# Second attention: half of each head's exponentials are added up on GpSimd before VectorE sums them

## The chip, the cores and the metric

The kernel runs on one core of a Trainium2 chip. The metric is the device time of one execution in microseconds (us). A core has five engines that run in parallel, each through its own queue in order: TensorE (PE), VectorE (DVE), ScalarE (ACT), GpSimd (POOL) and SyncE (SP, used for DMAs). They wait for each other through semaphores.

## The reference

A small transformer over x of shape (2, 1024, 256) with a context of 77 rows of 192: a first cross attention, a feed-forward with a token-dependent part, a **second cross attention**, and a mixture of 8 experts that each pick 257 tokens of a batch. Each stage normalises x and adds its result to it. The change concerns the softmax of the second attention:

```python
q = (x @ Wq).reshape(B, Sq, h, d).transpose(0, 2, 1, 3)      # h = 8 heads, d = 64
k = (context @ Wk).reshape(B, -1, h, d).transpose(0, 2, 1, 3) # 77 keys
scores = jnp.einsum('bhid,bhjd->bhij', q, k) * scale
attn = jax.nn.softmax(scores, axis=-1)
out = jnp.einsum('bhij,bhjd->bhid', attn, v)
```

## The kernel before

The 2048 rows of x are 16 tiles of 128 rows. In the second attention a tile n has 8 x 77 = 616 scores per row. Keys and query weights are multiplied together beforehand (`WK`), as are values and output weights (`VW`), so a tile goes through these steps:

1. TensorE, `scores(n)`: 12 products into the PSUM banks 4 and 5, which it may overwrite when VectorE has signalled `v_sub` for tile n-1.
2. VectorE, `scores(n)`: the maximum of each head (L1617), then the subtraction into `Pb[n % 3]` (L1621), which signals `v_sub`.
3. ScalarE, `exps(n)`: the exponential in place (L2232), signals `a_exp`.
4. VectorE, `normed(n)`: the sum of each head's 77 exponentials (L1626) and its reciprocal (L1628), signals `v_rec`.
5. GpSimd, `normed(n)`: multiplies the 616 exponentials by the reciprocals (L2541), signals `g_pb`.
6. TensorE transposes the tile in five pieces (L880) into banks 6 and 7; ScalarE copies the high part out (L1973) and VectorE the rest (L1653).
7. TensorE, `product(n)`: 15 products with `VW`; VectorE adds the result to x (L1634) and takes its statistics (L1636).

Each engine's program is a Python generator, `attention1(g)` for the four tiles of group g. `scores`, the exponential and `normed` run two tiles ahead of the transposes. The function `merge` interleaves the side work into this order, a piece after so many steps: the transposed queries of the next group (`queries`, L1486 on VectorE), the routing of finished tiles (`route_norm`: statistics to mean and variance, L1598 to L1602 on VectorE, a power on GpSimd, L2467, and a product, L2532, then the normalised rows, L1218 on VectorE; `route_pick`: router products L920, a small softmax, L1688 to L1699, and the splitting of the scores into pieces on GpSimd, L2595 to L2603), and in group 0 the routing constants (`constants`, L1706 to L1715 on VectorE and L2560 to L2583 on GpSimd). The order is fixed when the program is built. For GpSimd it is, around the multiplications (m0 to m15): m0, m1, first constants, m2, two iotas, the rest of the constants (which wait for VectorE's L1715), m3 to m6, power and product of routing group 0, m7, m8, m9, splitting of group 0, m10, power and product of group 1, m11, m12, m13, splitting, m14, power and product, m15. For VectorE a tile's turn is maximum and subtraction of tile n+2, L1653 of tile n, addition and statistics of tile n-1, sum and reciprocal of tile n+2.

Of the kernel before, what the change touches and what calls it, by code (L numbers as in the profile page):

```python
# [11 lines left out]
ALU = mybir.AluOpType  # L12
ACT = mybir.ActivationFunctionType
AX = mybir.AxisListType
# [5 lines left out]
H1 = 8  # L20
# [75 lines left out]
def build(nc, A, out, y_dram):  # L96
    with ExitStack() as root:
        def sem(name):
            return root.enter_context(nc.semaphore(name))
# [108 lines left out]
        s3 = Arena(R0.at)  # L208
# [5 lines left out]
        sm = s3("sm", [128, 3, 3, 8])  # L214
# [4 lines left out]
        s3 = Arena(qa_at)  # L219
# [3 lines left out]
        Pb = [s3(f"Pb{i}", [128, 640]) for i in range(3)]  # L223
        PT1 = [[s3(f"PTx{i}{j}", [128, 5, 128], F32R) for j in range(2)] for i in range(2)]
        wr_at = nc.sbuf_usable_end // 64 * 64 - 16384
        yr2 = s3("yr2", [128, 4, D])
        xf2 = s3("xf2", [128, 2, 512])
        assert s3.at <= wr_at


# [107 lines left out]
        g_pb = sem("g_pb")  # L338
# [93 lines left out]
        a_exp = sem("a_exp")  # L432
# [24 lines left out]
        def tensor_program(pe):  # L457
# [8 lines left out]
            def clear(b):  # L466
                if busy[b]:
                    pe.wait_ge(*busy[b])
                    busy[b] = None

            def warm(m, n):

                clear(m)
                for _ in range(n):
                    pe.transpose(bank[m][:, 0:128], ident[:, :], ident[:, :])  # L475
# [360 lines left out]
            def scores(n):  # L836
                g, t = n // 4, n % 4
                b, c = g // 2, 512 * (g % 2) + 128 * t
                clear(4)
                clear(5)  # L840
                if t == 0:
                    pe.wait_ge(v_xt, 2 * (8 + g) + 2)
                if n == 0:
                    pe.wait_ge(v_wk, 8)
                for u in range(2):
                    w_ = slice(308 * u, 308 * u + 308)
                    op = three(bank[4 + u][:, 0:308], [((xt[0][:, k, c:c + 128], xt[1][:, k, c:c + 128]),
                                                        (WK[0][:, b, k, w_], WK[1][:, b, k, w_])) for k in range(2)])
                op.then_inc(p_s, 1)
                busy[4] = busy[5] = (v_sub, n + 1)  # L850

            def product(n):
                b, T, m = n // 8, PT1[n % 2], 1 + n % 2
                K = [128, 128, 128, 128, 104]
                clear(m)
                pe.wait_ge(v_pT, n + 1)
                if n == 0:
                    pe.wait_ge(v_vw, 6)
                three(bank[m][:, 0:256], [((T[0][0:K[c], c, :], T[1][0:K[c], c, :]),
                                           (VW[0][0:K[c], b, c, :], VW[1][0:K[c], b, c, :])) for c in range(5)]).then_inc(p_pv, 1)  # L860
                busy[m] = (v_x1, n + 1)

            def attention1(g):
                if g == 0:
                    scores(0)
                    warm(1, 10)
                    scores(1)
                    yield
                    yield
                for t in range(4):  # L870
                    n = 4 * g + t
                    if n + 2 < NT:
                        scores(n + 2)
                    yield
                    clear(6)
                    clear(7)
                    pe.wait_ge(g_pb, n + 1)
                    o = ps[:, 6:8, :].rearrange("p u n -> p (u n)")
                    for c in range(5):
                        op = pe.transpose(o[:, 128 * c:128 * c + 128], Pb[n % 3][:, 128 * c:128 * c + 128], ident[:, :])  # L880
                    op.then_inc(p_pT, 1)
                    busy[6] = busy[7] = (v_pT, n + 1)
                    yield
                    if n:
                        product(n - 1)
                        yield
                    yield
                if g == 3:
                    product(NT - 1)
# [124 lines left out]
            drain(sd, vw_)  # L1014
            sd = queries(1, q_)
            merge(attention1(0), (sd, 0.6))
            drain(sd)
            for g in range(1, 3):
                qs = queries(g + 1, q_)
                rs_ = both(idle(6 if g == 1 else 3), route_norm(g - 1), idle(3 if g == 1 else 6), route_pick(g - 1, (0,), 0, 0))  # L1020
                merge(attention1(g), (qs, 0.6), (rs_, 1.0))
                drain(qs, rs_)
            rs_ = both(idle(3), route_norm(2), idle(8), route_pick(2, (0, 3), 0, 3))
            merge(attention1(3), (rs_, 1.0), (both(idle(12), route_norm(3)), 1.0))
            last_routes(rs_, route_norm(4), route_pick(3, (4,), 7, 4), route_pick(4, (5,), 6, 5))

# [162 lines left out]
        def vector_program(v):  # L1189
            made = {"st": 0, "unit": 0}  # L1190

            def step(op):

                op.then_inc(v_st, 1)
                made["st"] += 1

            def settle():
                v.wait_ge(v_st, made["st"])
# [424 lines left out]

            def normed(n):
                v.wait_ge(a_exp, 144 + n + 1)
                step(v.tensor_reduce(sm[:, n % 3, 1, :], Pb[n % 3][:, 0:616].rearrange("p (h s) -> p h s", h=H1), AX.X, ALU.add))  # L1626
                settle()
                v.reciprocal(sm[:, n % 3, 2, :], sm[:, n % 3, 1, :]).then_inc(v_rec, 1)  # L1628

# [8 lines left out]
            def attention1(g):  # L1638
                if g == 0:
                    scores(0)  # L1640
                    scores(1)
                    yield
                    normed(0)
                    normed(1)
                    yield
                src = ps[:, 6:8, :].rearrange("p u n -> p (u n)")[:, 0:640].rearrange("p (c n) -> p c n", c=5)
                for t in range(4):
                    n = 4 * g + t
                    if n + 2 < NT:
                        scores(n + 2)  # L1650
                    yield
                    v.wait_ge(a_pT, n + 1)
                    v.tensor_tensor(PT1[n % 2][1][:, :, :], src, f(PT1[n % 2][0][:, :, :]), ALU.subtract).then_inc(v_pT, 1)  # L1653
                    yield
                    if n:
                        product(n - 1)
                        yield
                    if n + 2 < NT:
                        normed(n + 2)
                    yield  # L1660
                if g == 3:
                    product(NT - 1)
# [790 lines left out]
        def gpsimd_program(g_):  # L2453
            made = {"st": 0}

            def step(op):

                op.then_inc(g_st, 1)
                made["st"] += 1
# [77 lines left out]

            def normed(n):
                pbh = Pb[n % 3][:, 0:616].rearrange("p (h s) -> p h s", h=H1)
                g_.wait_ge(v_rec, n + 1)  # L2540
                g_.tensor_tensor(pbh, pbh, sm[:, n % 3, 2, :].unsqueeze(2).to_broadcast([128, H1, SC]), ALU.mult).then_inc(g_pb, 1)  # L2541

            def attention1(g):
                if g == 0:
                    yield
                    normed(0)
                    normed(1)
                    yield
                for t in range(4):
                    n = 4 * g + t  # L2550
                    yield
                    yield
                    if n:
                        yield
                    if n + 2 < NT:
                        normed(n + 2)
                    yield
# [393 lines left out]
```

## Time and profile before

| | us |
|---|---|
| median of 3 runs | 821.63 (821.62 to 821.73) |
| the profiled execution's own time | 820.28 |
| its span, first to last instruction | 818.2 |
| PE busy | 758.7 (93%) |
| DVE busy | 529.2 (65%) |
| ACT busy | 399.3 (49%) |
| POOL busy | 322.0 (39%) |

The mean granted TensorE clock was 0.978 of full speed. The second attention runs from about 466 to 552 us. The shares over the whole span are averages over stages with different limits. The rows further down are from views of this stage.

### The profile page before, as it was taken

How to read it: one execution, taken by the hardware profiler on the slowest of the kernel's cores; microseconds unless marked ns; L12 is line 12 of the kernel's file. 1: busy time of each engine (PE TensorE's matmuls, PEld its weight loads, DVE VectorE, ACT ScalarE, POOL GpSimd, SP SyncE). 2: the span in 40 equal slices, each digit the busy share in tenths (PEclk: the TensorE clock that was granted, in tenths of full speed). 3: DMA queues.
4: the chain of work that ended last, by engine and by line, in shares of the span. 5: the costliest groups of instructions: out<-in, count | busy, mean ns of one | idle time of the engine just before them, and what ended most of it. 6: DMA issues, size and time to landing. Idle time of an engine off the chain costs nothing.

```text
span 818.2 us, 12847 instructions
## 1 busy us (share of the span) xinstructions
PE 758.7 (93%) x4881; PEld 620.0 (76%) x4881; DVE 529.2 (65%) x1163; ACT 399.3 (49%) x699; POOL 322.0 (39%) x281
## 2 busy tenths in 40 slices
PE   8889999999999999999999989994689999999995
PEld 8655556656755564679889888883689999999995
DVE  7767875773677683357455498885747655667552
ACT  3655643573466344563472245433035765557650
POOL 6502002100201022066361143334336878888793
PEclk9999999999999999999999999996799999999998
DMA  7000000000000100100030201111212545544432
GB/s 186 2 1 1 1 1 1 1 1 1 1 1 1 52 4 0 52 1 3 1 98 2 103 2 52 53 65 52 104 29 83 144 109 151 145 99 127 126 33 32
DMA packets 21509, 39.31 MB, mean 48 GB/s; under 512 B 4913, under 2 KB 16905, under 8 KB 19145
## 3 DMA queue, kind: packets, MB, share of 16 engines
q1 hardware_dynamic: 14793, 30.07, 11.1%
q0 software_dynamic: 6656, 8.43, 5.9%
q8 instruction: 39, 0.64, 0.3%
q14 instruction: 21, 0.17, 0.1%
HBM read 29.96 MB, written 8.40 MB: 47 GB/s over the span
## 4 chain that ended last, share of the span: by engine, by line
PE 56%; DVE 14%; ACT 4%; issue 3%; POOL 3%; DVEq 0%; ACTq 0%
PE ps L481 18%; PE ps L650 8%; PE ps L1173 6%; PE ps L1176 5%; PE ps L754 5%; PE ps L671 2%; PE ps L672 2%; PE ps L612 2%; PE ps L475 1%; DVE rep L1811 1%; DVE sm L1617 1%; PE ps L1096 1%; DVE Pb L1621 1%; POOL out_dram L2733 1%; DVE sm L1626 1%
## 5 line engine op out<-in xcount | busy, mean ns | idle before, releaser
L650 PE MATMUL ps<-PT,VA 128*65 128x512 f32 (+1 forms) x288 | 147.9, 595 | 3.6 <-ACT PT L2120 3.3
L2120 ACT ACTIVATE PT<-ps 128x512 f32<-128x512 f32 x128 | 76.1, 595 | 71.0 <-PE ps L672 70.8
L481 PE MATMUL ps<-GT,wh 128*128 128x258 f32 (+1 forms) x768 | 94.7, 284 | 0.4 <-DVE GT L1909 0.4
L481 PEld LDWEIGHTS ps<-GT,wh 128*128 128x128 f32 x768 | 92.7, 189 | 0.6 <-DVE GT L1909 0.6
L2733 POOL DMA_INDIRECT out_dram<-ye,idx x40 | 69.7, 1743 | 19.8 <-issue 10.9
L2417 ACT ACTIVATE het<-ps,b1e 128x514 f32<-128x514 f32 x64 | 44.3, 692 | 58.4 <-PE ps L481 54.0
L1944 DVE TENSOR_TENSOR he<-het,he 128x514 fp32r<-128x514 f32 x64 | 46.4, 726 | 35.6 <-ACT he L1973 35.1
L671 PE MATMUL ps<-QA,KA 128*128 128x512 f32 x144 | 67.7, 470 | 0.8 <-ACT QB L1973 0.8
L2467 POOL TENSOR_TENSOR rs<-rs,half 128x4 f32<-128x4 f32 (+2 forms) x19 | 18.2, 958 | 119.7 <-DVE rs L1214 91.3
L2477 POOL TENSOR_TENSOR ssq<-ssq,half 128x8 f32<-128x8 f32 x12 | 19.7, 1638 | 108.3 <-DVE ssq L1295 108.3
L2611 POOL DMA_INDIRECT gt<-y_dram,idx x40 | 46.4, 1159 | 40.2 <-DVE gate L1899 30.4
L612 PE MATMUL ps<-KA,QA 128*128 128x368 f32 x192 | 59.1, 413 | 3.0 <-ACT mrt L1973 0.8
L612 PEld LDWEIGHTS ps<-KA,QA 128*128 128x128 f32 x192 | 33.4, 188 | 36.9 <-DVE x L1423 15.6
L650 PEld LDWEIGHTS ps<-PT,VA 128*65 128x65 f32 (+1 forms) x288 | 38.5, 138 | 29.2 <-ACT PT L2120 9.8
L1409 DVE TENSOR_REDUCE mxp<-ps 128x1 f32<-128x736 f32 x64 | 58.5, 914 | 0.2 <-PE ps L612 0.2
L1407 DVE TENSOR_REDUCE mxp<-ps 128x1 f32<-128x368 f32 x64 | 34.5, 539 | 36.5 <-PE ps L612 35.6
L672 PE MATMUL ps<-QB,KB 65*128 65x512 f32 x144 | 57.1, 397 | 0.0
L1173 PE MATMUL ps<-he,wh 128*128 128x258 f32 x384 | 54.8, 291 | 0.6 <-DVE he L1944 0.6
L481 PE MATMUL ps<-wo,OT 65*128 65x258 f32 x192 | 53.3, 386 | 0.2 <-DVE x L1423 0.2
L481 PEld LDWEIGHTS ps<-wo,OT 65*128 65x128 f32 x192 | 31.2, 189 | 27.8 <-issue 24.5
L754 PE MATMUL ps<-w2e,hT 128*128 128x256 f32 x384 | 50.5, 286 | 0.0
L1176 PE MATMUL ps<-wh,he 128*128 128x256 f32 x384 | 50.2, 284 | 0.0
(291 smaller groups left out, 1662.8 us busy)
## 6 DMA issues: line engine op xcount, KB each, us to landing
wr<-in_w1e_dram SPq DMA_DIRECT2D x8, 1024.0 KB, 5.1
wr<-in_w2e_dram SPq DMA_DIRECT2D x8, 1024.0 KB, 4.9
x<-in_x_dram SPq DMA_DIRECT2D x4, 512.0 KB, 6.7
w<-in_w_dram SPq DMA_DIRECT2D x2, 1024.0 KB, 4.7
y_dram<-yr SPq DMA_DIRECT2D x3, 512.0 KB, 3.0
out_dram<-x SPq DMA_DIRECT2D x3, 512.0 KB, 4.1
b2r<-in_b2r_dram SPq DMA_DIRECT2D x8, 128.0 KB, 3.1
gt<-y_dram,idx POOLq DMA_INDIRECT x40, 3.0
```

Source lines behind the costliest of these rows:

```text
L481: op = pe.matmul(o, l, r, start=n == 0, stop=n == len(calls) - 1)
L612: op = pe.matmul(ps[:, j, 0:368], QA[:, h, 128 * qt:128 * qt + 128], KA[:, h, 368 * j:368 * j + 368], start=True, stop=True)
L650: pe.matmul(bank[6 + hf][0:65, :], VA[b][0:K, kt, h, :], PT[u % 4][0:K, :], start=kt == 0, stop=kt == 8).then_inc(p_pv, 1)
L671: pe.matmul(bank[m][0:K, :], KA[:, h, ks], QA[:, h, qc], start=True, stop=False)
L672: pe.matmul(bank[m][0:K, :], KB[:, h, ks], QB[:, h, qc], start=False, stop=True).then_inc(p_s, 1)
L754: op = pe.matmul(bank[bk][:, 0:256], l, r, start=n == 0, stop=n == 23)
L1173: op = pe.matmul(bank[dc][:, 0:258], w2h[i][:, wc_], he[j][:, m, 256:514], start=n == 0, stop=n == 23)
L1176: op = pe.matmul(bank[dc][:, 0:256], he[j][:, m, c0:c0 + 128], w2h[i][:, 256 * m:256 * m + 256], start=n == 0, stop=n == 23)
L1409: v.tensor_reduce(mxp[:, qt, 0:1], ps[:, 0:2, 0:368], AX.XY, ALU.max).then_inc(v_mx, 1)
L1944: v.tensor_tensor(he[1][:, m, :], het[m % 2][:, :], f(he[0][:, m, :]), ALU.subtract).then_inc(v_he, 1)
L2120: a.activation(PT[u % 4][0:K, :], bank[4 + u % 2][0:K, :], ACT.Exp, bias=0.0 if K == 128 else mcol[:, b:b + 1]).then_inc(a_exp, 1)
L2733: g_.indirect_dma_start(out, bass.IndirectOffsetOnAxis(ap=idx[0:M, ex, s_:s_ + 1], axis=0), ye[ex % 2][0:M, s_, :], None, compute_op=ALU.a ...
```

## The change

GpSimd adds the exponentials 38 to 75 of each head to its exponentials 0 to 37 and copies the last one, number 76, into a new buffer `half_sums` of 39 columns a head (two buffers, used in turn). VectorE's sum reads these 39 columns in place of the 77. GpSimd's two new instructions stand before the multiplication of the same tile, wait for the exponential, and signal `g_pb`; so `g_pb` counts two steps a tile, VectorE waits for the odd ones, and TensorE's wait is for the even ones.

```diff
@@ -225,6 +225,7 @@
+        half_sums = [s3(f"half_sums{i}", [128, H1, 39]) for i in range(2)]
@@ -874,7 +875,7 @@
-                    pe.wait_ge(g_pb, n + 1)
+                    pe.wait_ge(g_pb, 2 * n + 2)
@@ -1623,7 +1624,8 @@
             def normed(n):
                 v.wait_ge(a_exp, 144 + n + 1)
-                step(v.tensor_reduce(sm[:, n % 3, 1, :], Pb[n % 3][:, 0:616].rearrange("p (h s) -> p h s", h=H1), AX.X, ALU.add))
+                v.wait_ge(g_pb, 2 * n + 1)
+                step(v.tensor_reduce(sm[:, n % 3, 1, :], half_sums[n % 2][:, :, :], AX.X, ALU.add))
                 settle()
                 v.reciprocal(sm[:, n % 3, 2, :], sm[:, n % 3, 1, :]).then_inc(v_rec, 1)
@@ -2537,6 +2539,9 @@
             def normed(n):
                 pbh = Pb[n % 3][:, 0:616].rearrange("p (h s) -> p h s", h=H1)
+                g_.wait_ge(a_exp, 144 + n + 1)
+                g_.tensor_tensor(half_sums[n % 2][:, :, 0:38], pbh[:, :, 0:38], pbh[:, :, 38:76], ALU.add)
+                g_.tensor_copy(half_sums[n % 2][:, :, 38:39], pbh[:, :, 76:77]).then_inc(g_pb, 1)
                 g_.wait_ge(v_rec, n + 1)
                 g_.tensor_tensor(pbh, pbh, sm[:, n % 3, 2, :].unsqueeze(2).to_broadcast([128, H1, SC]), ALU.mult).then_inc(g_pb, 1)
```

## Rows read from the trace of the kernel before

**Rows 1.** Busy by window: start:end, length, PE, PEld, DVE, ACT, POOL, clock, DMA.
```profile
485.00:495.00 10.00, 10.00 (x82) 10.00 (x80) 9.22 (x18) 4.94 (x9) 2.44 (x2) 1.00 0.01 2
...
475.00:545.00 70.00, 63.33 (x489) 61.45 (x490) 63.76 (x140) 29.97 (x50) 25.56 (x41) 0.99 0.09 32
```

**Rows 2.** Groups of PE, 475 to 545: busy, mean ns, idle before and releaser.
```profile
L481 PE MATMUL ps<-WK,xt 128*128 128x308 f32 x156 | 25.0, 309 | 4.5 <-DVE Pb L1621 4.4
```

**Rows 3.** Groups by form, whole kernel, POOL and DVE: busy, mean ns.
```profile
L2541 POOL TENSOR_TENSOR Pb<-Pb,sm 128x616 f32<-128x616 f32 x16 | 19.5, 1223 | 44.1 <-DVE sm L1628 44.1
...
L2597 POOL TENSOR_TENSOR gres<-sc,vals 128x32 f32<-128x32 f32 x3 | 0.8, 262 | 0.2
...
L2603 POOL CAST vals<-gres 128x16 bf16<-128x16 f32 x2 | 0.5, 238 | 0.1
...
L1693 DVE TENSOR_REDUCE ss<-lg 128x4 f32<-128x32 f32 x3 | 0.6, 187 | 0.9 <-ACT lg L2288 0.9
```

**Rows 4.** Timeline of an undisturbed tile (4): start, us, engine, line.
```profile
484.60 0.72 ACT L2232 ACTIVATE Pb<-Pb 128x616 f32<-128x616 f32 x1 [1.07 <-DVE Pb L1621]
...
486.01 0.78 DVE L1626 TENSOR_REDUCE sm<-Pb 128x8 f32<-128x616 f32 x1
...
486.94 0.75 DVE L1617 TENSOR_REDUCE sm<-ps 128x8 f32<-128x616 f32 x1
```

**Rows 5.** Timeline of the start, tiles 0 to 2.
```profile
472.20 0.74 DVE L1626 TENSOR_REDUCE sm<-Pb 128x8 f32<-128x616 f32 x1
...
472.36 2.40 POOL L2541 TENSOR_TENSOR Pb<-Pb,sm 128x616 f32<-128x616 f32 x2 [4.97 <-DVE sm L1628]
...
473.66 0.79 DVE L1617 TENSOR_REDUCE sm<-ps 128x8 f32<-128x616 f32 x1
```

**Rows 6.** Timeline around tile 3 and the routing constants.
```profile
480.44 0.17 DVE L1715 TENSOR_TENSOR cj<-io 128x10 int32<-128x10 int32 x1
...
482.05 0.78 DVE L1626 TENSOR_REDUCE sm<-Pb 128x8 f32<-128x616 f32 x1
...
482.68 0.62 POOL L2583 CAST vals<-io 128x128 bf16<-128x128 int32 x1
```

**Rows 7.** Timeline around tile 7 and the first routing group.
```profile
500.47 0.16 DVE L1602 TENSOR_SCALAR rs<-mv 128x4 f32<-128x4 f32 x1
500.54 0.79 DVE L1626 TENSOR_REDUCE sm<-Pb 128x8 f32<-128x616 f32 x1
500.71 1.02 POOL L2467 TENSOR_TENSOR rs<-rs,half 128x4 f32<-128x4 f32 x1 [3.25 <-DVE rs L1602]
...
501.96 1.29 POOL L2541 TENSOR_TENSOR Pb<-Pb,sm 128x616 f32<-128x616 f32 x1
502.09 0.80 DVE L1617 TENSOR_REDUCE sm<-ps 128x8 f32<-128x616 f32 x1
...
503.87 1.92 PE L481 MATMUL ps<-WK,xt 128*128 128x308 f32 x12 [1.10 <-DVE Pb L1621]
```

**Rows 8.** Chain of waits around tile 10: start, us, engine and line.
```profile
511.30 1.81 PE ps L481 x12
513.13 0.81 DVE sm L1617
```

**Rows 9.** Timeline: exponential 11, a normalisation, and L1601 beside GpSimd.
```profile
521.42 0.72 ACT L2232 ACTIVATE Pb<-Pb 128x616 f32<-128x616 f32 x1 [2.12 <-DVE Pb L1621]
...
522.36 0.40 DVE L1218 TENSOR_SCALAR yr<-x,mv,rs 128x256 f32<-128x256 f32 x1
...
539.58 1.04 DVE L1601 TENSOR_SCALAR nmr<-mv 128x4 f32<-128x4 f32 x1
```

**Rows 10.** Timeline of PE behind a gap; then a window: PE busy, granted clock, DMA.
```profile
543.38 1.04 PE L880 MATMUL ps<-ident,Pb 128*128 128x128 f32 x5 [1.92 <-DVE PTx L1653]
...
544.08 3.36 PE L481 MATMUL ps<-VW,PTx 128*128 128x256 f32 x15
...
544.00:545.00 1.00, 1.00 (x7) 0.50 0.13 44
```

## The prediction

> **What bounds the kernel now.** Only the second attention changes, so I read that stage: first the busy time in windows, then the chain of waits, then the order of each engine in time. Between 475 and 545 us VectorE is busy 63.8 of 70 us and TensorE 63.3; in the ten microseconds from 485 TensorE is busy for all ten [rows 1]. Neither engine has room. In the rest of the stage VectorE carries side work (the query and routing pieces) and TensorE waits for it: all but 0.1 us of the 4.5 us that the score products waited in the window was for the subtraction at L1621, which frees their banks [rows 2]. That wait is what a lighter VectorE could win back. GpSimd is busy 25.6 us of the 70 [rows 1], yet its queue is in order, and today VectorE never waits for it in `normed`.
>
> I write M, R and S for a tile's maximum (L1617), its sum (L1626) and its score products (L481), with the number of the tile. All times below are starts in the profiled execution.
>
> **Part 1, what is removed.** R reads 616 elements and takes 0.78 us [rows 4]. A reduction of 32 elements to 4 takes 0.187 us [rows 3]. On the line between the two, 312 elements take about 0.47 us, so each R gets 0.31 us shorter; sixteen of them make 4.9 us of VectorE work. The bounds are 0.19 and 0.78 us, for a saving of 0.59 and of nothing.
>
> **Part 2, what is added.** GpSimd gets an addition of 8 x 38 elements and a copy of 8. Its two-input operation costs 1.223 us for 616 elements and 0.262 us for 32 [rows 3], which puts 304 elements at 0.71 us (bounds 0.26 and 1.22). For the copy I take 0.20 us, below the 0.238 us of a cast of 16 elements [rows 3] (bounds 0 and 0.24). Less some overlap of the two, and with a hand-over (a GpSimd operation starts 0.08 us after the VectorE operation it waits for ends: 500.47 + 0.16 to 500.71 [rows 7]), R can begin about 0.91 us after the addition begins, if nothing is ahead of it in GpSimd's queue. The bounds of this delay are 0.4 and 1.5 us.
>
> **Part 3, the undisturbed tile.** The exponential of tile 4 ends at 485.32, R4 starts at 486.01 (0.69 us later) and M5 0.93 us after that [rows 4]. Now R may begin at 485.32 + 0.08 + 0.91 = 486.3 and M5 follows 0.62 us later, at 486.9, where it is today. The loop maximum, subtraction, exponential, addition, shorter sum closes in the same time: the shorter sum is paid back as the wait for GpSimd. Tiles 4, 5, 12 and 14 give nothing. Behind the waiting R stand the reciprocal and the next M, and behind that M the bank release for TensorE.
>
> **Part 4, where GpSimd's queue is in the way.** The addition of tile n stands directly before the multiplication of tile n, so behind everything that is queued ahead of that multiplication. Three places matter.
> - Start. R1 runs at 472.20, before the multiplication of tile 0 is over. Now the addition of tile 1 is queued behind it. The pair of multiplications started at 472.36 and takes 1.20 us each [rows 5]; the first starts 0.3 us earlier because R0 is shorter, and ends at 473.26. R1 then starts at 473.26 + 0.91 = 474.17, and M2 (1.46 us behind R1 in the trace, 1.18 with the shorter R) at 475.35 instead of 473.66 [rows 5]: **+1.7**. R2 is not delayed and gives 0.3 back: +1.4.
> - Tile 3. GpSimd makes the routing constants between the multiplications of tiles 2 and 3; they start after the VectorE shift at 480.44 and end at 482.68 + 0.62 = 483.30, while R3 runs at 482.05 [rows 6]. With 1.4 us of lateness the addition starts at 484.7, R3 at 485.6, and M4 0.62 us later at 486.2 instead of 482.98: **+3.25** in all, 1.85 of them new. VectorE's product and statistics are all ahead of R3, so nothing fills the wait.
> - Tile 7. VectorE issues the variances at 500.47 and R7 at once at 500.54; GpSimd does the power from 500.71 and the product behind it, and its tile 7 multiplication starts at 501.96 [rows 7]. There the addition will start. With +3.25 that is 505.2, R7 at 506.1, and M8 after R7, the reciprocal and one normalisation (0.95 us) at 507.07 against 502.09 [rows 7]: **+5.0** in all, 1.7 new.
>
> **Part 5, what is won back.** R6 gives nothing, because VectorE waits there for ScalarE's query copy, which moves with TensorE. After S9 (503.87, which waited 1.10 us for VectorE) the chain runs through TensorE until S10 ends at 513.11 and M10 starts at 513.13 [rows 7, 8], so R8 and R9 give nothing. R10 and R11 give 0.31 each. Against them stands a new collision: the addition of tile 11 starts 0.08 us after the exponential (521.42 + 0.72), the second normalisation at L1218 is due at 522.36 [rows 9]. A VectorE operation on a scalar that meets GpSimd at work was held until GpSimd ended: L1601 took 1.04 us at 539.58 [rows 9], while its neighbour L1602, of the same form, takes 0.16 [rows 7]. With the present lateness of 4.7 against 4.65 the two coincide, and the normalisation waits about 0.55 us. So +4.97 - 0.31 + 0.55 - 0.31 = **+4.9**, and S13 to M14 is again a chain through TensorE, so nothing is recovered. The next steps (experts) only start later.
>
> The Trainium skill, "GPSIMD Engine Reference", section Key points, says that GpSimd shares its memory interfaces with VectorE instructions that read through both ports. The row of L1601 agrees. By that rule the sum is 4.9; read without it, it is 4.35.
>
> **Part 6, the clock.** Each stall opens a gap on TensorE: after the query transposes at 474.9 until S3 at 477.1 (2.2 us), from 486.0 to S5 at 488.0 (2.0 us), from 506.0 to S9 at 508.85 (2.8 us). The trace has one gap of that size: 1.92 us before 543.38, and behind it the granted clock is 0.50, which is 1.2 GHz instead of 2.4. The 5 transposes there took 1.04 us and the 15 products 3.36 [rows 10]; elsewhere in the stage they take 0.71 and 2.03, so 1.66 us were lost. A gap like the 1.10 us before 503.87 [rows 7] did not do it: the mean clock of the window is 0.99 with that one fall in it [rows 1]. The first gap would be absorbed by the wait at tile 3; the second and third fall on work that TensorE itself bounds, 1.66 us each. I take one of the two: **+1.7**. The bounds are 0 and 3.3.
>
> **Sum.** 4.9 + 1.7 = 6.6 us on the profiled execution: 820.28 (span 818.2 and 2.1 around it) becomes 826.9. That execution lies 1.35 us below the median of the timed runs, 821.63, so the predicted median is 828.2.
>
> **Rivals.**
> - *The clock decides otherwise.* With no drop 821.6 + 4.9 = 826.5, with two 829.9. Same mechanism, inside my range.
> - *Hidden after all.* The stalls fall where TensorE has slack and the shorter sums repay them. For it: TensorE had some 6.7 us idle in the window [rows 1]. Against it: at tiles 1, 3 and 7 the chain of waits runs through VectorE. If the waits at tiles 3 and 7 cost half (1.8 in place of 3.6), the start 1.2, and R9 to R15 give 0.31 each (2.2) with no clock loss, the time is 822.4, within 0.2%.
> - *Faster.* This is decided at L1621: the score products wait 4.5 us for it [rows 2]. If GpSimd's addition is near its lower bound and VectorE does its waiting where it idles today, each R pays 0.31 us wherever VectorE leads, at most the 4.5 us; less 1.2 us at the start and 0.9 at tile 3 that gives 819.2. It decides when the delay behind the exponential is under 0.6 us; the 1.22 us row speaks against so cheap an addition.
> - *A dear addition.* If the split rows of 38 cost as much as the whole row, the delay is 1.5 us and each of nine waits is 0.6 longer: 828.2 + 5.4 = 833.6.
>
> **Chances.** Forecast with its clock variants 0.76; dear addition 0.08; hidden 0.10; faster 0.06. This gives faster (by over 0.2%, 1.6 us, about what a measurement can tell from no change) 0.05, within it 0.10, slower 0.85. The range is 824.2 to 831.0: from the cheap end of the addition (0.5 off each of three stalls, no collision and a little on undisturbed tiles, about 2.3 below 826.5) to two clock drops with a delay of 1.0 us.
>
> **What would show it.** VectorE waits for GpSimd before L1626 of tiles 1, 3 and 7 by some 2 us each, and by 0.2 to 0.3 on the undisturbed tiles; L1626 at 0.47 us; the new addition at 0.71 us and copy at 0.20; the last M15 about 4.9 us later than 540.61 before the clock; the granted clock at 0.50 once or twice between 488 and 515. I am wrong if the addition of tile 3 doesn't stand behind the constants, if the gaps leave the clock alone, or if undisturbed tiles get shorter.

## The result, and the profile after

The changed kernel takes 828.35 us (median of 5 runs, 825.6 to 831.99) against 821.63; the ratio is 1.0084, with a 95% interval of 1.0069 to 1.0099. It is slower by 6.9 us (5.7 to 8.1) by the ratio, 6.7 by the medians. The profiled execution took 828.16 us, its span is 826.4.

The first view is the busy time of the same window as in [rows 1], of the changed kernel (columns as there):

```profile
475.00:545.00 70.00, 61.71 (x459) 60.30 (x460) 56.70 (x128) 26.90 (x45) 35.81 (x65) 0.95 0.09 31
```

VectorE is 7 us less busy in the seventy, GpSimd 10 us more, and TensorE is 1.6 us less busy although the work of a tile is the same for it: the window holds fewer tiles. The granted clock is 0.95 in place of 0.99. The waits of the stage (engine and line, whom it waited for: us in total, times, longest) say where:

```profile
POOL half_sums L2543 <- ACT Pb L2234: 14.4, 13, 2.2
...
PE ps L482 <- DVE Pb L1622: 10.3, 8, 2.9
DVE sm L1628 <- POOL half_sums L2544: 7.1, 7, 2.3
```

The last row is new: VectorE waits seven times for the halves, 7.1 us in all, for work that became 16 x 0.3 = 4.8 us shorter. The groups of the new and changed instructions (busy, mean ns, idle before):

```profile
L2543 POOL TENSOR_TENSOR half_sums<-Pb 128x304 f32<-128x304 f32 x16 | 11.7, 732 | 14.4 <-ACT Pb L2234 14.4
...
L2544 POOL COPY half_sums<-Pb 128x8 f32<-128x8 f32 x16 | 3.3, 208 | 0.0
```

```profile
L1628 DVE TENSOR_REDUCE sm<-half_sums 128x8 f32<-128x312 f32 x16 | 7.5, 471 | 7.1 <-POOL half_sums L2544 7.1
```

Three of the seven waits make most of it. The timeline of VectorE in the changed kernel shows them at tiles 1, 3 and 7, against [rows 5 to 7], with the ordinary one at tile 4 (L1618 behind a sum is the maximum of the next tile):

```profile
474.39 0.48 DVE L1628 TENSOR_REDUCE sm<-half_sums 128x8 f32<-128x312 f32 x1 [2.23 <-POOL half_sums L2544]
...
485.65 0.48 DVE L1628 TENSOR_REDUCE sm<-half_sums 128x8 f32<-128x312 f32 x1 [1.54 <-POOL half_sums L2544]
...
486.29 0.75 DVE L1618 TENSOR_REDUCE sm<-ps 128x8 f32<-128x616 f32 x1
...
489.67 0.48 DVE L1628 TENSOR_REDUCE sm<-half_sums 128x8 f32<-128x312 f32 x1 [0.28 <-POOL half_sums L2544]
...
490.31 0.75 DVE L1618 TENSOR_REDUCE sm<-ps 128x8 f32<-128x616 f32 x1
...
506.39 0.48 DVE L1628 TENSOR_REDUCE sm<-half_sums 128x8 f32<-128x312 f32 x1 [2.32 <-POOL half_sums L2544]
```

GpSimd's timeline gives the reason. Before tile 1's addition stands the multiplication of tile 0, before tile 3's the last cast of the routing constants, before tile 7's the power and a product of 0.20 us at 505.26. The exponentials of these tiles had ended at 472.29, 482.64 and 502.61:

```profile
472.24 1.22 POOL L2546 TENSOR_TENSOR Pb<-Pb,sm 128x616 f32<-128x616 f32 x1 [2.77 <-DVE sm L1630]
473.42 0.72 POOL L2543 TENSOR_TENSOR half_sums<-Pb 128x304 f32<-128x304 f32 x1
...
484.35 0.62 POOL L2588 CAST vals<-io 128x128 bf16<-128x128 int32 x1
484.68 0.73 POOL L2543 TENSOR_TENSOR half_sums<-Pb 128x304 f32<-128x304 f32 x1
...
504.15 1.03 POOL L2469 TENSOR_TENSOR rs<-rs,half 128x4 f32<-128x4 f32 x1 [3.57 <-DVE rs L1603]
...
505.41 0.74 POOL L2543 TENSOR_TENSOR half_sums<-Pb 128x304 f32<-128x304 f32 x1
```

And TensorE's timeline has the gap before the score products of tile 9, and the products behind it at half the clock:

```profile
509.07 3.35 PE L482 MATMUL ps<-WK,xt 128*128 128x308 f32 x12 [2.85 <-DVE Pb L1622]
```

```profile
510.00:512.00 2.00, 2.00 (x10) 0.50 0.20 69
```

(The second fence is a view of windows: start:end, length, PE busy, granted clock, DMA; 0.50 is 1.2 GHz. From 508 to 510 us the clock is 0.79 in the mean, from 512 to 514 it is 0.86.)

To compare kernels I use milestones from the timelines: the start of the maximum of tile n less that of tile 0. They take out whatever the earlier stages did. One profiled execution each, us; the labels are those of the experiments below:

| kernel | M2 | M4 | M8 | M10 | M12 | M15 |
|---|---|---|---|---|---|---|
| before | 7.70 | 17.02 | 36.13 | 47.17 | 58.44 | 74.65 |
| after | 9.44 | 20.15 | 41.16 | 53.48 | 64.45 | 80.67 |
| after, again | 9.43 | 20.13 | 41.13 | 53.16 | 64.13 | 80.35 |
| early_1 | 8.39 | 19.10 | 40.10 | 53.33 | 64.31 | 80.53 |
| early_3 | 9.44 | 18.78 | 39.86 | 50.64 | 61.62 | 77.83 |
| early_7 | 9.42 | 20.57 | 39.83 | 50.64 | 61.61 | 77.83 |
| early_all | 8.38 | 17.14 | 36.69 | 47.47 | 58.44 | 74.66 |
| early_every | 8.39 | 17.24 | 36.80 | 47.59 | 58.57 | 74.79 |
| filler_9 | 9.42 | 20.13 | 41.15 | 51.94 | 62.92 | 79.14 |
| add_unused | 7.69 | 17.24 | 36.37 | 47.73 | 59.40 | 75.64 |
| add_twice | 10.10 | 21.74 | 44.91 | 56.94 | 68.07 | 86.25 |
| sum39_alone | 7.50 | 16.20 | 35.19 | 45.96 | 56.59 | 72.46 |
| defer_before | 7.69 | 17.62 | 38.06 | 49.09 | 61.86 | 78.40 |
| defer_all | 8.40 | 18.52 | 38.39 | 49.15 | 61.71 | 77.95 |

From before to after: +1.74, +3.13, +5.03 at M2, M4 and M8, +6.31 at M10 and +6.02 at M15. From the start of the last tile's statistics to the end of the span there are 265.3 us before and 267.3 after; that part is taken up below.

### The profile page after: what moved, and what is told of

Its sections match the earlier page's. It is cut to its first block, busy times and chain, and to the rows that moved or that the text cites. A ratio compares the mean times of both kernels' runs of the same rounds, so it can differ in the third digit from the quotient of the medians.

```text
span 826.4 us, 12895 instructions
## 1 busy us (share of the span) xinstructions
PE 762.1 (92%) x4881; PEld 622.8 (75%) x4881; DVE 524.1 (63%) x1163; ACT 397.9 (48%) x699; POOL 337.0 (41%) x313
## 4 chain that ended last, share of the span: by engine, by line
PE 55%; DVE 13%; ACT 4%; issue 4%; POOL 3%; another core or an unknown queue 0%; DVEq 0%; ACTq 0%
PE ps L482 18%; PE ps L651 8%; PE ps L1174 5%; PE ps L1177 5%; PE ps L755 5%; PE ps L672 2%; PE ps L673 2%; PE ps L613 2%; DVE sm L1618 1%; DVE rep L1813 1%; PE ps L1097 1%; DVE Pb L1622 1%; POOL out_dram L2738 1%; ACT htmp L2183 1%; PE ps L823 1%
```

## Experiments

Each run was timed beside the kernel before on the same chip; a difference in us is the ratio's, on 821.6.

**The three places together** (early_all; n + 2 is the tile whose scores are worked on). GpSimd's `normed` is split in `halved` (addition and copy, with a semaphore `g_hs` of their own) and the multiplication:

```diff
+                    halved(0)
+                    halved(1)
                     normed(0)
                     normed(1)
...
                     yield
+                    if n + 2 in (3, 7):
+                        halved(n + 2)
                     yield
                     if n:
                         yield
                     if n + 2 < NT:
+                        if n + 2 not in (3, 7):
+                            halved(n + 2)
                         normed(n + 2)
```

> The changed kernel with GpSimd's addition and copy moved ahead in its queue at three places: tile 1 before the multiplication of tile 0, tile 3 before the routing constants, tile 7 before the power of the first routing group (a semaphore of its own for the halves). Theory 1 (the loss is made by the place in GpSimd's queue at these three tiles, and by the clock that falls behind the gaps on TensorE): three waits of about 2 us before L1626 go, the granted clock stays at 1.00 between 478 and 515 us, and about 6 of the 6.7 us come back: 821.3, between 820.3 and 822.5. Theory 2 (the loss is a wait and contention spread over all sixteen tiles, 0.4 us each): less than 2 us come back, 826 or more.

Measured: ratio 0.9988 (0.9973 to 1.0002), 1.0 us under the kernel before (2.2 under to 0.2 over), so the whole loss is gone; a gain isn't shown. The granted clock of its profile is 1.00 in every window from 466 to 545 us. The waits of the stage:

```profile
POOL half_sums L2544 <- ACT Pb L2235: 17.8, 15, 2.9
...
DVE sm L1629 <- POOL half_sums L2545: 2.6, 5, 1.2
```

7.1 us of waiting for the halves became 2.6. GpSimd now waits for the exponential 15 times instead of 13, and no more stands behind other work where it matters. Theory 1 holds, theory 2 doesn't. M15 is at 74.66 against 74.65: the stage is as long as before, no shorter.

**Each place alone.**

> Only tile 7's addition is moved ahead, before the power. Theory 1: the new part of the wait at tile 7 (1.7 us) goes, and with it the gap of 2.85 us on TensorE before the scores of tile 9 and the fall of the clock there (1.3 to 1.7 us): 828.35 - 3.2 = 825.2. If the clock fell for another reason, only 1.7 come back: 826.7. Theory 2: within 0.5 us of the changed kernel.

> Only the first two tiles: GpSimd adds the halves of tiles 0 and 1 before it multiplies tile 0. Theory 1: the maximum of tile 2 comes 1.2 us earlier than in the changed kernel (the wait at tile 1 shrinks to some 0.9 us), the gap on TensorE before the scores of tile 3 too, so the clock doesn't fall there; the wait at tile 3 stays behind the constants. 1.2 us less than the changed kernel run beside it. Theory 2 (the wait of each tile counts the same): 0.4 us less.

> Only tile 3's addition is moved ahead of the routing constants. Theory 1: the wait of 1.5 us before that sum goes and the maximum of tile 4 comes 1.85 us earlier; 1.8 us less than the changed kernel run beside it, if TensorE, slowed by the clock before tile 4, doesn't take its place (then 0.5 to 1.0 less). Theory 2: 0.4 us less.

early_7 (`if n + 2 in (7,)` alone; tile 1's addition is again behind the multiplication of tile 0, in early_3 too): ratio 1.0036 (1.0019 to 1.0054), +3.0 us where the changed kernel has +6.9. That is 3.9 less, where theory 1 with the clock said 3.2; M4 to M8 shrinks from 21.0 to 19.3, the 1.7 us of the wait, and M8 to M10 from 12.3 to 10.8, the 1.5 us of the clock. Its M4 is 0.4 later than in the changed kernel: in this execution the clock fell further behind the first gap (0.51 from 478 to 484 us; 0.72 in the changed kernel), and the wait at tile 3 didn't cover all of it.

early_3 (`in (3,)`): 1.0040 (1.0027 to 1.0053), +3.3 us, against +6.7 for the changed kernel beside it. I expected 1.8 less and it was 3.4. M4 to M15 shows how: M4 is 1.37 earlier (TensorE was slow there, 0.79 between 478 and 484 us), and the rest is again M8 to M10, 10.8 instead of 12.3. In this execution the same gap before tile 9 didn't drop the clock.

early_1 (the first two added lines of the diff): 1.0071 (1.0048 to 1.0094), 0.8 us less than the changed kernel beside it, with an interval from 2.7 less to 1.1 more; so the timed runs leave it open. M2 is 1.05 us earlier (1.2 expected), and the later maxima stay so until M8; then M8 to M10 takes 13.2 us, the clock having been at 0.59 between 508 and 516. Its runs lie apart as this suggests: 824.89 and 825.83 us, with mean clocks of 0.981 and 0.977 over the whole execution, and four from 829.83 to 830.71, all with 0.971.

**The changed kernel again**, beside these:

> The changed kernel once more, as the measure for the three that run beside it on the same chip. Both theories: 6.7 us over the kernel before, within 1.

1.0081 (1.0068 to 1.0094), +6.7 us. The milestones agree with the first profile to 0.03 us up to M8, although here the clock was at 1.00 behind the first two gaps on TensorE (2.57 and 1.75 us) and fell only behind the third (2.86 us).

**The clock.**

```diff
+                    if n + 2 == 9:
+                        warm(1, 22)
                     if n + 2 < NT:
                         scores(n + 2)
```

> The changed kernel with 22 transposes of the identity (about 2.3 us) on TensorE in the gap of 2.85 us before the scores of tile 9, into a bank that is free; nothing waits for them. Theory 1 (the gap drops the clock, and the clock makes 1.3 us of the loss): the granted clock between 508 and 516 us stays at 1.00, the 12 score products take 1.93 us again in place of 3.35, and 1.3 us are saved against the changed kernel run beside it. Rival (the clock falls for another reason, or something else bounds that stretch): no gain, or 0.2 us of loss.

The timeline of TensorE with the filler (L476 is the filler):

```profile
504.49 2.57 PE L476 MATMUL ps<-ident 128*128 128x128 f32 x22
507.50 1.92 PE L482 MATMUL ps<-WK,xt 128*128 128x308 f32 x12 [0.45 <-DVE Pb L1624]
```

The products took 1.92 us instead of 3.35 and M8 to M10 10.8 instead of 12.3. So the fall of the clock costs 1.5 us here (1.2 against after_again), besides the gap itself. The timed ratio is 1.0049 (1.0032 to 1.0067) against 1.0081: 2.6 us less, more than the 1.3 expected. That the filler kept the clock isn't proven by one profile, because early_3 kept it through the same gap without a filler; the timed runs speak for it. In this profile the clock is at 1.00 until 556 us, so the fall at [rows 10] is missing too; but it is missing in after_again as well. Whether the filler also makes later falls rarer, the profiles can't say.

**GpSimd's work without VectorE's wait.** The halves are computed and not used:

```diff
-                v.wait_ge(g_pb, 2 * n + 1)
-                step(v.tensor_reduce(sm[:, n % 3, 1, :], half_sums[n % 2][:, :, :], AX.X, ALU.add))
+                step(v.tensor_reduce(sm[:, n % 3, 1, :], Pb[n % 3][:, 0:616].rearrange(...), AX.X, ALU.add))
...
+                g_.wait_ge(g_pb, 2 * n + 1)
                 g_.wait_ge(v_rec, n + 1)
```

> The changed kernel's addition and copy on GpSimd stay where they are, but VectorE sums the 77 exponentials as before and doesn't wait for GpSimd (the halves aren't used). Theory 1: GpSimd's work costs nothing unless VectorE waits for it; the multiplications come up to 0.9 us later, which TensorE's transposes have slack for except at the start (0.5 us), and the normalisations beside the additions of tiles 11 and 15 wait 0.3 us: 822.3 (821.4 to 823.2). Theory 2 (contention): every VectorE step beside an addition gets longer, and more than half of the 6.7 us stays: above 825.

1.0005 (0.9993 to 1.0016): +0.4 us, between 0.6 under and 1.3 over. GpSimd's 15 us of added work cost next to nothing (1.0 us at M15 in the profile), even with the long sum back on VectorE; the loss is in the waiting.

**The shorter sum for nothing.** The kernel before, summing columns 0 to 38 of each head and leaving out the other 38:

```diff
-  ...rearrange("p (h s) -> p h s", h=H1), AX.X, ALU.add))
+  ...rearrange("p (h s) -> p h s", h=H1)[:, :, 0:39], AX.X, ALU.add))
```

> The kernel before, with VectorE summing only the first 39 exponentials of each head and nothing on GpSimd (the other 38 are left out of the sum). It shows what the shorter sum is worth if the other half cost nothing. Theory 1: L1626 takes 0.47 us, 0.31 less, but TensorE bounds the undisturbed tiles and the chains through it at tiles 10 and 14, so of 16 x 0.31 = 5.0 us only about 2 come through: 819.6 (818.5 to 820.8). Rival: VectorE bounds the whole stage and all 5 us come through: 816.7.

0.9961 (0.9947 to 0.9976): 3.2 us less, between my 2 and the rival's 5. On 821.6 that is 818.4 us, just under the 818.5 that I gave as the lower bound. By milestones it is 0.8 us by M4, 0.9 by M8, 1.9 by M12, 2.2 at M15 and 3.0 at the last tile's statistics. Between M4 and M8, where the undisturbed tiles are, it is 0.1: M4 to M5 is 0.26 us shorter, and the next tiles give half of it back. So TensorE leaves next to nothing there. What I had too low is the end, behind M15, where I had counted nothing.

**A dearer addition.** A second addition into a buffer that isn't read:

```diff
+                g_.tensor_tensor(half_sums2[n % 2][:, :, 0:38], pbh[:, :, 0:38], pbh[:, :, 38:76], ALU.add)
```

> The changed kernel with GpSimd's addition done twice (the second into a buffer that isn't read), so each sum's delay behind the exponential grows by 0.67 us. Theory 1: the waits at tiles 1, 3 and 7 grow by 0.67 each, as do those of the undisturbed tiles 4, 5, 12 and 14, and tile 8 begins to wait; 4.7 to 6 us over the changed kernel, so 11.5 to 13 over the kernel before. Rival (only the three queue places matter): 2 us over the changed kernel.

1.0153 (1.0133 to 1.0174), +12.6 us over the kernel before and 5.9 over the changed one. That is within the 4.7 to 6 of theory 1, and about nine times the 0.67 us of more delay. By the milestones the distance to the changed kernel grows by 0.6 to 0.8 us at each of M2, M4, M5, M6, M8, M13, M14 and M15. So the delay of the halves is on the path at many tiles, and the undisturbed tile has no room for a later sum. (The clock fell at other places than in the changed kernel, behind gaps of 2.45 and 3.53 us, so not every tenth belongs to the addition.)

**All additions early.** `halved` after the first `yield` of every tile:

> The additions of all tiles moved ahead in GpSimd's queue, not of three alone. Theory 1: the other tiles' additions already waited for the exponential and for nothing in GpSimd's queue, so this equals early_all: 1.5 to 2 us under the kernel before, and the waits of 0.2 to 0.3 us on tiles 4, 5 and 12 stay. Rival (the queue delays every tile a little): another 1 us or more off early_all.

1.0005 (0.9994 to 1.0015), +0.4 us where I had expected 1.5 to 2 under the kernel before: the size missed. The wait for the halves is 2.6 us in 5 waits, exactly as in early_all; M15 differs by 0.13. So the order at the other tiles isn't shown to make a difference, as theory 1 said. That early_all came out 1.0 us under and this 0.4 over the kernel before I can't tell from chance; neither is shown to be faster.

**Sum behind the next subtraction.** On VectorE `normed(n + 1)` follows `scores(n + 2)`, with and without the change:

```diff
                     if n + 2 < NT:
                         scores(n + 2)
+                    if 2 <= n + 1 < NT:
+                        normed(n + 1)
                     yield
...
-                    if n + 2 < NT:
-                        normed(n + 2)
                     yield
```

> The three additions moved ahead as in early_all, and VectorE takes the sum and reciprocal of a tile only behind the next tile's maximum and subtraction, so that GpSimd's addition has that time to land. Theory 1 (on undisturbed tiles the loop maximum, subtraction, exponential, addition, sum holds the period, and the shorter sum is paid back as a wait of 0.3 us): no wait for the halves is left, each sum's 0.31 us comes through where VectorE leads, and the time reaches what the shorter sum was worth alone, 3 us under the kernel before. Rival: the multiplications come 1.5 us later and TensorE's transposes now wait for GpSimd; the gain over early_all is nothing or a loss.

> The kernel before with the same move of sum and reciprocal behind the next maximum and subtraction, and nothing else. Theory 1: VectorE has the same work and waits for nothing in normed, so the move alone gives nothing (within 0.7 us). Rival: the score products get their banks back earlier by the 0.9 us of sum and reciprocal, and the move alone makes the gain: 2 us or more under the kernel before.

Both expectations missed: defer_all 1.0089 (1.0074 to 1.0104), +7.3 us, defer_before 1.008 (1.0063 to 1.0096), +6.6. At the undisturbed tile the theory held for one tile only: in defer_all the maximum follows that of the tile before after 3.75 us (483.02 to 486.77) against 4.02 in the changed kernel, but the next follows after 4.21, having waited 0.48 for TensorE's products. One wait for the halves is left. The loss is elsewhere. At M15 defer_before is 3.75 us behind the kernel before, and at the last tile's statistics 7.1; defer_all is 3.3 and 7.2 behind. Defer_all's waits from 480 to 552 us:

```profile
PE ps L882 <- DVE PTx L1658: 7.9, 3, 4.0
DVE yr L1220 <- POOL rs L2470: 5.8, 3, 2.3
```

The normalisation of a routing group waits for GpSimd's power, and in the kernel before the sum lies in between: there this wait is 0.2 us in all. The transposes wait 7.9 us for L1658 instead of 1.9. In defer_before the same two waits are 5.7 and 8.3 us. A sum that seemed to be in the way was filling a gap: that is my reading of these waits, and no run puts something else in its place. The clock has a part too (0.84 in defer_before and 0.69 in defer_all between 545 and 556 us, 0.91 in the kernel before).

## Why the prediction was right

The median was put at 828.2 us and is 828.35; slower had a chance of 0.85, faster 0.05. The mechanism was the forecast one. That the number came out so close is luck, as the last step shows. Step by step:

- **The prices.** The shorter sum was put at 0.47 us, measured 0.471; the addition 0.71, measured 0.732; the copy 0.20, measured 0.208. For the sum and the addition, interpolating between two rows of the same operation was enough; the copy was a guess below the row of a cast.
- **The three places** (part 4). Predicted +1.7, +3.25, +5.0 at M2, M4, M8; measured +1.74, +3.13, +5.03. early_all shows that the order in GpSimd's queue is the cause, early_7 and early_3 that places 7 and 3 each carry a part. For tile 1 only the milestones of early_1 show it. add_unused shows that it is the wait, and not GpSimd's load.
- **The undisturbed tile** (part 3) was put at no change. It became 0.06 us longer (M4 to M5 is 4.02, before 3.96 from 482.98 to 486.94), with the forecast wait of 0.28. The sum began 0.97 us after the addition (484.68 to 485.65), where I had 0.91: that is the 0.06. add_twice shows the delay of the addition on the path there. That TensorE leaves no gain there held nearly: without any wait for GpSimd, sum39_alone is 0.1 us shorter from M4 to M8, and the 0.27 that defer_all gains at one tile is mostly lost at the next.
- **What is won back** (part 5). I had nothing between M8 and M10 before the clock; in filler_9 and early_7, at full clock there, it is 0.2 us less than in the kernel before. The second normalisations beside the additions of tiles 11 and 15 took 0.74 us instead of 0.40: the collision is there, 0.34 us where I had 0.55. M10 to M12 gained 0.3 on balance, I had 0.1.
- **The clock** (part 6). I took one fall of 1.7 us for the second and third of three gaps. In the profiled execution the clock fell behind the first (0.72 from 478 to 484 us) and behind the third, worth 1.5 us against filler_9. The first was absorbed at tile 3 as forecast: after_again kept 1.00 there and has the same M4. The second gap was only 0.80 us long because the first fall had made TensorE late; in after_again it was 1.75. The price of a fall is shown. Whether one comes isn't fixed by the gap: early_3 kept its clock through the same third gap, and early_1 paid 2.4 us. So one fall was a draw that came out. The changed kernel's runs spread over 6.4 us, those of the kernel before beside it over 1.7. The slowest (831.99) has a mean clock of 0.971 over the whole execution and the fastest (825.6) 0.980, as falls of the clock would make it; in which stage they fell the timed runs can't say.
- **The sum of the stage** is 6.0 at M15, predicted 4.9 + 1.7 = 6.6. Without a fall behind the third gap it is 4.5 (filler_9, 79.14 against 74.65) where I had 4.9, and the fall is 1.5 where I had 1.7.
- **Behind the stage** I had counted nothing. The span is 8.2 us longer, 826.4 against 818.2 (the profiled execution as a whole 7.9), and 2.0 of that lie behind the last tile's statistics. With some 1.3 of them goes one wait in the first expert:

```profile
627.62 0.59 PE L1097 MATMUL ps<-ident,gt 128*128 128x128 f32 x3 [1.30 <-DVE GT L1911]
```

Just ahead of it, until 625.34, ScalarE stood still for 1.56 us for a releaser that the profile only calls remote. The same wait of TensorE, 1.3 to 1.4 us long, stands in the profiles of after_again, early_1, early_3, early_every, filler_9, add_twice, defer_all and defer_before, and not in those of early_7, early_all, add_unused, sum39_alone and the kernel before. From the last tile's statistics to the end the nine with the wait take 266.7 to 269.9 us, the five without it 265.0 to 266.5. early_all and early_every, with the same stage, are on both sides, and defer_before has the wait with no new work on GpSimd at all. So it doesn't follow from the change alone, and what makes it stays open.

- **The luck.** The profiled execution was put at 826.9 and took 828.16: 0.6 too much for the stage and 2.0 missing behind it. I then added 1.35 us because the kernel before's profiled execution lies that far below its median; the changed kernel's lies 0.2 below. These misses nearly cancel, and the median comes out 0.1 from the forecast.

## What to carry to other kernels

Work that is moved to an idle engine is priced by its place in that engine's queue, not by its duration: read what is queued ahead of it at each irregular place, and who will now stand behind it. Moving three additions ahead of work that is needed later cost nothing here and gave back all 6.9 us. And an instruction that looks like load on the bound engine may be the filler of a wait: leaving out 0.3 of the sum's 0.78 us in each of 16 tiles was worth 3.2 us in all, and moving the sum cost 6.6.

## What the runs showed of the hardware

- A gap of 2.85 us on TensorE was followed by a clock of 0.50 in the changed kernel and by a full one in early_3, whose timeline of TensorE has the same wait in the same place, and the products at 1.92 us instead of 3.35:

```profile
506.24 1.92 PE L483 MATMUL ps<-WK,xt 128*128 128x308 f32 x12 [2.85 <-DVE Pb L1623]
```

With the gap filled, the clock was 1.00 in the one profile of filler_9. Against filler_9's 10.8 us from M8 to M10, a fall in this stretch cost between 1.2 and 2.4 us.

- The same gap did or didn't bring a fall from one execution to the next. Behind the gap of 2.85 us the clock fell in three profiles (after, after_again, early_1) and not in early_3. Behind the first gap, 2.57 us, it fell in after, early_3 and early_7 and not in after_again and filler_9; in add_twice it stayed at 1.00 behind a first gap of 3.25 us and fell behind one of 2.45.

- A VectorE instruction on one tensor and scalars took longer beside a GpSimd instruction: L1219 0.74 us beside the new additions (528.52 beside the one at 528.38, 549.40 beside the one at 549.26), 0.36 to 0.42 otherwise. The stage's two-input and reducing instructions of VectorE that read scores or products from PSUM kept their mean durations: L1655 814 ns (814 before), L1622 800 (799), L1618 777 (774).
